# Softmax probabilities of the second attention: scaled by the reciprocal sums on GpSimd and then transposed, in place of products with diagonal matrices

## What is computed

```python
qh = (q @ w_q.T).reshape(b, n, H, D_K).transpose(0, 2, 1, 3)
kh = (k @ w_k.T).reshape(b, n, H, D_K).transpose(0, 2, 1, 3)
vh = (v @ w_v.T).reshape(b, n, H, D_V).transpose(0, 2, 1, 3)
scores = jnp.einsum('bhid,bhjd->bhij', qh, kh) / math.sqrt(D_K)
scores = jnp.where(causal[None, None], scores, -jnp.inf)
attn = jax.nn.softmax(scores, axis=-1)
out = jnp.einsum('bhij,bhjd->bhid', attn, vh)
out = out.transpose(0, 2, 1, 3).reshape(b, n, H * D_V)
x = x + out @ w_o.T
```

## Time and profile before

| | us |
|---|---|
| median of 3 runs | 2098.38 |
| lowest and highest run | 2093.04 and 2102.99 |
| the profiled execution | 2091.37 |
| its span, first to last instruction | 2089.5 |
| TensorE busy (matmul), weight load busy | 1612.6 and 1376.6 |
| VectorE, ScalarE, GpSimd busy | 860.5, 555.8, 300.4 |

### The profile page before, as it was taken

One profiled execution on the slowest core, in us unless ns is written; L12 is line 12 of the kernel. 1 busy time (PEld: TensorE's weight loads), 2 busy tenths in 40 slices (PEclk: granted clock), 3 DMA queues, 4 the chain that ended last, 5 costly groups with the idle time before them and its releaser, 6 DMA issues. The chain is left out here.

```text
span 2089.5 us, 33168 instructions
## 1 busy us (share of the span) xinstructions
PE 1612.6 (77%) x11474; PEld 1376.6 (66%) x11474; DVE 860.5 (41%) x1977; ACT 555.8 (27%) x1375; POOL 300.4 (14%) x337
## 2 busy tenths in 40 slices
PE   2799997449971899999997069999999436692665
PEld 2565664449971788888887069999999424481654
DVE  5443543402215455554554301111111243648896
ACT  1233232102212444444442011111111011131553
POOL 1121120110002222121210500000000320004122
PEclk8899999579995999999997579999999768896688
DMA  4444350266213000000002254244452111011000
GB/s 125 58 76 63 51 72 4 69 237 231 94 55 129 6 7 6 7 6 2 1 1 99 75 204 143 88 146 146 143 203 86 51 58 30 28 30 41 6 16 21
DMA packets 118235, 152.11 MB, mean 73 GB/s; under 512 B 15360, under 2 KB 101376, under 8 KB 118016
## 3 DMA queue, kind: packets, MB, share of 16 engines
q1 hardware_dynamic: 101536, 123.86, 19.4%
q0 software_dynamic: 7680, 18.89, 4.1%
q10 hardware_dynamic: 8928, 8.13, 1.1%
HBM read 113.16 MB, written 24.64 MB: 66 GB/s over the span
## 5 line engine op out<-in xcount | busy, mean ns | idle before, releaser
L1268 PEld LDWEIGHTS f_ph<-f_xgT,f_w 128*128 128x128 f32 x3232 | 373.5, 193 | 20.3 <-issue 16.2
L1268 PE MATMUL f_ph<-f_xgT,f_w 128*128 128x128 f32 x3232 | 374.5, 276 | 15.7 <-DMA f_w<-in_f_w 15.5
L1278 PE MATMUL f_py<-f_w,f_hT 128*128 128x256 f32 x992 | 224.6, 379 | 0.2 <-ACT f_hT L1308 0.2
L1278 PEld LDWEIGHTS f_py<-f_w,f_hT 128*128 128x128 f32 x992 | 183.6, 190 | 23.2 <-issue 0.8
L1339 DVE TENSOR_TENSOR f_hT<-f_ph,f_gate_o 128x512 f32<-128x512 f32 x78 | 53.9, 691 | 309.9 <-ACT f_gate_o L1302 309.9
L795 ACT ACTIVATE a_work<-a_ps,a_bias 128x128 f32<-128x128 f32 (+1 forms) x256 | 104.0, 418 | 139.6 <-DVE a_bias L875 132.5
L1373 POOL DMA_INDIRECT c_yt<-sorted_y,dest x48 | 45.5, 947 | 649.8 <-issue 648.6
L145 PE MATMUL n_tp<-ident,n_xn 128*128 128x128 f32 x160 | 32.5, 377 | 134.7 <-DVE n_xn L125 134.0
L1302 ACT ACTIVATE f_gate_o<-f_ph 128x512 f32<-128x512 f32 x78 | 46.6, 597 | 295.2 <-PE f_ph L1268 295.1
L145 PEld LDWEIGHTS n_tp<-ident,n_xn 128*128 128x128 f32 x160 | 25.1, 192 | 142.5 <-DVE n_xn L125 135.6
L932 POOL TENSOR_TENSOR a_diag<-ident,a_recip 128x512 f32<-128x512 f32 x64 | 66.6, 1040 | 338.4 <-DVE a_recip L890 338.4
(11 more groups left out here) (309 smaller groups left out, 3078.1 us busy)
## 6 DMA issues: line engine op xcount, KB each, us to landing
f_w<-in_f_w SPq DMA_DIRECT2D x72, 1024.0 KB, 7.1
f_xg<-sorted_x SPq DMA_DIRECT2D x62, 128.0 KB, 2.1
sorted_y<-f_yg ACTq DMA_DIRECT2D x62, 128.0 KB, 1.7
a_qs<-a_part SPq DMA_DIRECT2D x96, 64.0 KB, 5.6
a_ks<-a_part POOLq DMA_DIRECT2D x96, 64.0 KB, 5.7
sorted_x<-zeros SPq DMA_DIRECT2D x1, 4992.0 KB, 16.2
a_ctxT<-in_ctxT SPq DMA_DIRECT2D x16, 256.0 KB, 2.7
sorted_x<-zeros SPq DMA_DIRECT2D x1, 2944.0 KB, 10.2
```

The source lines that it names most:

```text
L1268: mm = pe.matmul(ph[:, q, n, f * P:(f + 1) * P], w[:, s, k, (q * FQ + f) * P:(q * FQ + f + 1) * P], xgT[:, s, k, :], start=(k == 0), stop= ...
L1278: mm = pe.matmul(py[:, s, 0:D], hT[:, s, f, :], w2[:, s, f, :], start=(f == 0), stop=(f == FT - 1))
```

## The change

The scaling moves from TensorE's product to the probabilities themselves. GpSimd no longer writes diagonal matrices. In their place it multiplies the unit's probabilities in `prob` by the reciprocals, in place, with one instruction for the first 128 queries (two heads, 128 columns) and one for the others (two heads, 256 columns). TensorE's six products with diagonal matrices become six transposes with the identity. The semaphore `diag_done`, one count for a unit, becomes `shares_done` with two counts. The buffer `diag` goes. GpSimd's own wait for `t_ready` goes; the probabilities of a slot are already kept from being overwritten before the turn has read them, by ScalarE's wait for `t_ready`.

```diff
-        diag = sb("diag", [P, 2, TB * 2, P])
...
             def turn(pair, u):
                 s = u % 2
-                pe.wait_ge(diag_done, upto(pair, u))
+                pe.wait_ge(shares_done, upto(pair, u, TB))
                 if u >= 1:
                     pe.wait_ge(t_out0, upto(pair, u - 1))
                     pe.wait_ge(t_out1, upto(pair, u - 1))
                 for i in range(2):
-                    for n, t in enumerate((0, 1, 1)):
-                        mm = pe.matmul(ps[:, TB_ + i, n * P:(n + 1) * P], prob[:, s, i, n * P:(n + 1) * P],
-                                       diag[:, s, 2 * t + i, :], start=True, stop=True)
+                    for n in range(3):
+                        mm = pe.transpose(ps[:, TB_ + i, n * P:(n + 1) * P], prob[:, s, i, n * P:(n + 1) * P],
+                                          consts["ident"][:, :])
                 mm.then_inc(t_ready, 1)
...
                 dve.wait_ge(exp_done, upto(pair, u, 4))
                 if u >= 2:
-                    dve.wait_ge(diag_done, upto(pair, u - 2))
+                    dve.wait_ge(shares_done, upto(pair, u - 2, TB))
                 dve.reciprocal(recip[:, s, :, :], total[:, s, :, :]).then_inc(recip_done, 1)
...
-            def diagonals(pair, u):
+            def shares(pair, u):
+
                 s = u % 2
                 pool.wait_ge(recip_done, upto(pair, u))
-                if u >= 2:
-                    pool.wait_ge(t_ready, upto(pair, u - 2))
-                pool.tensor_tensor(diag[:, s, :, :], consts["ident"][:, :].unsqueeze(1).to_broadcast([P, 2 * TB, P]),
-                                   recip[:, s, :, :].rearrange("p t i -> p (t i)").unsqueeze(2
-                                                                                  ).to_broadcast([P, 2 * TB, P]),
-                                   ALU.mult).then_inc(diag_done, 1)
+                for t in range(TB):
+                    part = prob[:, s, :, t * P:(P if t == 0 else TRI)]
+                    pool.tensor_tensor(part, part, recip[:, s, t, :].unsqueeze(2).to_broadcast([P, 2, P * (t + 1)]),
+                                       ALU.mult).then_inc(shares_done, 1)
```

More of the change, by code:

```diff
@@ L607, in attention1 @@
          ctx_in0, ctx_in1, src_high, src_split, q_proj, k_proj, v_proj, q_high, k_high, q_low, k_low,
-         v_out, s_ready, max_done, bias_done, exp_done, recip_done, diag_done, t_ready, t_out0, t_out1, pv_done,
+         v_out, s_ready, max_done, bias_done, exp_done, recip_done, shares_done, t_ready, t_out0, t_out1, pv_done,
          o_high, o_low, wo_ready, resid_done) = (
@@ L613, in attention1 @@
                  "q_proj", "k_proj", "v_proj", "q_high", "k_high", "q_low", "k_low", "v_out", "s_ready",
-                 "max_done", "bias_done", "exp_done", "recip_done", "diag_done", "t_ready", "t_out0", "t_out1",
+                 "max_done", "bias_done", "exp_done", "recip_done", "shares_done", "t_ready", "t_out0", "t_out1",
                  "pv_done", "o_high", "o_low", "wo_ready", "resid_done"))
@@ L940, in step @@
                 if is_unit(n - SCORE):
-                    diagonals(pair, n - SCORE)
+                    shares(pair, n - SCORE)
                 if n % U == 2 and is_unit(n + 6):
```

## The result

The changed kernel takes 2063.4 us (median of 4 runs, 2062.1 to 2066.6), the kernel before 2095.7 (4 runs, 2092.7 to 2103.0). The ratio is 0.984 with a 95% interval of 0.981 to 0.987, so the change saves about 32 or 33 us. The forecast was 2063, and 35 us. In a second set of runs the ratio was 0.986 (0.984 to 0.988), so the third digit is not sure.

The account below looks back on a forecast made before the run. TensorE's issue pace was taken to bound the stage; savings of 30.6, 1.5, 2.0 and 0.8 us sum to 35, which taken from the median of 2098.4 gives 2063 us, with an 8-in-10 range of 2048 to 2076.

Parts of the forecast that it names:

- What is removed on TensorE: Each turn: six products become six transposes, 1.44 to 0.68 us, 48.6 us over 64 turns if TensorE never waits.
- What is late next: VectorE's 5.25 us loop outlasts TensorE's new 5.05 us step; mask products wait for exponentials, round 23.71 us, saving 2.6.
- The limit of 4.3 us: Time GpSimd's two scaling instructions may take before a turn waits; the pair was taken as 2.0 us, hidden.
- The step that failed: Rounds with the residual addition: one VectorE loop stretches to 5.80 us, adding 0.55 wait and leaving a saving of 2.06.
- the 30.6 I had: Saving in us over steps 9 to 61: 7 rounds at 2.61 and 6 with the residual addition at 2.06.
- The ramp: Steps before step 9, without output work, where VectorE's loop already is the longer: saving 1.5 us.
- what follows step 61: Three turns save 2.0 us, two or three steps after projections end give nothing, the last turn saves 0.8.
- The clock: New waits cost no clock; slower rival: transposes drop part of the stage to the lower level, 2100 or more, chance 0.05.
- TensorE keeps all of it: Rival: the 0.2 us waits don't form, saving 46 us, 2052 us, chance 0.15.
- the two passes: Rival: transposes cost two passes like the products, so only waits move, 2098 us, chance 0.05.
- GpSimd is late: Rival: GpSimd's pair takes over 4.3 us and turns wait for it, 2070 to 2095 us, chance 0.07.
- The contention rival: Five VectorE instructions beside GpSimd's pair take 0.25 us longer each, loop 6.5 us, 2103 (2075 to 2105), chance 0.05.

Follow-up runs that it names:

- The first experiment: Changed kernel with TensorE's transposes replaced by plain products with the identity, GpSimd's scaling kept: 2097.6 us, ratio 1.000 to the kernel before.
- The two VectorE copies: One unused 256-element VectorE copy out of PSUM added per step, to the kernel before (2099.9 us, ratio 1.002) and to the changed kernel (2081.5 us, 0.993).
- 3.2 (no wait in steady steps): Changed kernel with GpSimd's pair done twice, once into a buffer nobody reads, 3.2 us in place of 1.6: 2068.0 us, ratio 0.986.
- 4.8 (2089.8, with waits): Changed kernel with GpSimd's pair done three times, two into buffers nobody reads, 4.8 us in place of 1.6: 2089.8 us, ratio 0.996.
- the second profile: Profile of the changed kernel run once more, unchanged, in a further set: 2067.1 us, ratio 0.986, first to last turn 383.5 us.

## Why the prediction was right, and where its steps were off

The time was right, 2063 for 2063.4, and so was the mechanism: TensorE's step shortens by half of the turn, and VectorE's loop takes over as the limit. That the number fits to 0.4 us is luck. The saving was forecast as 35 us and is 32 by the medians and 30.3 from first to last turn, and the kernel before, from whose median of 2098.4 I subtracted, came out at 2095.7. Inside the sum, terms were off in both directions and cancelled in part.

- *What is removed on TensorE*: 384 records, a turn of 0.71 us for the 0.68 I took (0.65 and 0.72 were my bounds). The first experiment shows that it carries the whole gain. The register instruction costed at nothing cost nothing that can be seen: the step without waits is 5.08, and 5.81 less the 0.73 that the turn became shorter is 5.08.
- *What is late next*: the round of 23.71 came out at 23.73, its first step at 5.08 for 5.05, and its waiting step at 5.23 for 5.25. The waits stand at the mask products, for the exponentials. I had forecast 0.2 us some 40 times, 8 to 9 us in total; 37 waits of the weight loads and 10.7 us of idle matmul time were measured, or 19.1 us by the loads. The longer ones are those of the steps with a split, 1.21 us in the rows above. The two VectorE copies confirm that the limit has moved.
- *GpSimd*: the pair is 0.61 + 1.04, overlapping by little, 1.61 us in a row, where I took 2.0 between 1.56 and 2.58. Hidden, as said. The limit of 4.3 us agrees with 3.2 (no wait in steady steps) and 4.8 (2089.8, with waits).
- *The step that failed* is the one on VectorE in rounds with a residual: 2.06 us saved where the trace gives 26.3 - 25.3 = 1.0. I had the row, a bias of 0.41 us beside a split, and used it only to price a rival. Then I dismissed contention because the five VectorE instructions beside GpSimd's pair read PSUM. The sixth one, the bias, reads and writes SBUF, and it stands beside the split, not beside the pair. In the kernel before it already lasted 0.40 to 0.85 us at six splits, which cost nothing while TensorE set the pace. In the changed kernel it lies in the loop that sets the end, and it lasts 1.08 to 1.23. The shorter round does most of the lengthening (0.94 without GpSimd's pair), and the pair adds 0.2.
- *Where the 30.3 us come from*, by the starts of the turns in the two traces. From the turn of step 9 to that of step 61 it is 27.5 us for the 30.6 I had. Three rounds with residual and split lost 1.0 us each against the forecast. The first round, which has a split, took 25.49 for 23.71: 1.0 for the bias, and 0.7 in its value step, where VectorE's loop was still behind. Against these 4.8 us the two rounds over the back edges saved 3.6 and 2.4 us instead of 2.1 each. A part of it may be the clock: the kernel before drops to the lower level behind both back edges (0.51 from 845.0 to 848.5 us, 0.52 from 954.2 to 957.6), the changed one behind the second alone (0.50 from 935.3 to 938.7). I did not test this. The ramp gave 0.3 for 1.5 (1.2 in the second profile), and what follows step 61 gave 2.5 for 2.8.
- *The clock* stayed at 1.00, 1.00 and 0.98 with transposes in the stage. "TensorE: Matmul & The Clock Gate" of the Trainium skill says in Part 4 that transposes do not count as activity in the way matmuls do. Whether they count for less, no run here shows: with 0.7 us of transposes in a step of 5.1 the granted clock was not lower than the 1.00, 0.98 and 0.98 of the kernel before.

Of the rivals, "TensorE keeps all of it" falls by the waits and the copies, the two passes by 384 records, "GpSimd is late" by its one wait of 0.2 us. The contention rival had a real mechanism in another place and at about an eighth of its price (some 5 us for 40).

"GPSIMD Engine Reference" of the Trainium skill, Key points, names two kinds of VectorE instructions that collide with GpSimd, those with two SBUF inputs and those in a two-port mode. The bias can be of the second kind: "VectorE: DVE Perf Modes" of the Trainium skill, on the mode 2×_2P, says that a float32 operation of one tensor and a constant, SBUF to SBUF, can use both read ports. The traces agree as far as they go, 1.14 us beside GpSimd and 0.17 without; they show the wait, not the mode. They also show that it happens for four elements, and that the bias ends 0.02 to 0.03 us after the GpSimd instruction beside it in every run.

## What to carry to other kernels

In these traces a float32 product with a diagonal or an identity costs TensorE two records where a transpose costs one (1.44 us against 0.71 for six), so scaling belongs on an engine with room. Before such a trade, write down the loop of the engine that is next in line, from one instruction to the same one a step later: it told the new pace to 0.02 us in a round of 24 where nothing else collided, and showed what to move afterwards for another 8 to 12 us. A wait that costs nothing today, such as the bias beside the split, has to be priced anew once its engine becomes the limit. And when work is added to GpSimd, look at which SBUF-to-SBUF instruction of VectorE then stands beside what it pushes back.

## What the runs showed of the hardware

- A VectorE instruction of four elements, SBUF to SBUF with a constant, lasts until the GpSimd instruction beside it ends: 0.17 us alone, 0.40 to 0.85 beside the second subtraction of a split in the kernel before and 1.08 to 1.23 in the steady part of the changed one. Near the start of the stage it is GpSimd that is late, 2.72 us in place of 1.29 beside VectorE's subtraction of two SBUF operands, which had begun 0.7 us earlier.
- GpSimd scales 512 elements in place by a broadcast reciprocal in 1.04 us, as fast as it wrote the 512 elements of diagonals, and 256 in 0.61.
- Two runs of the same program in two sets differ by 3.7 us in the median (2063.4 and 2067.1), while their first-to-last distances differ by 0.8. The span less the first-to-last distance, the same code in all runs but for the edges of the stage, lies between 1675 and 1687 us over the profiles. A distance inside the trace tells apart what a median of such runs can't.
